# A fused decoder layer on one core: the output products of a pair of heads move between the next head's products, and the first loads and splits are reordered

## The reference

```python
x = x + attn(layernorm(x), W_K, W_Q, W_V, W_O)     # 16 heads of 128, b = 8, pos = 112, d = 512
x = x + xattn(layernorm(x), ctx, Wq, Wk, Wv)
x = x + ffn(layernorm(x), gate, experts, shared)

def attn(x, W_K, W_Q, W_V, W_O):
    k, q, v = (einsum('ihd,bpd->biph', W, x) for W in (W_K, W_Q, W_V))
    s = einsum('biph,biqh->biqp', k, q)
    p = softmax(where(tril, s, -1e10) / sqrt(128))
    z = einsum('biqp,biph->biqh', p, v)
    return einsum('df,bqf->bqd', W_O, z_flat)
```

## Time and profile before

| | us |
|---|---|
| median of 3 runs | 947.93 (947.91 to 949.11) |
| profiled execution, its own time | 951.71 |
| its span | 949.9 |
| PE busy in it | 912.1 (96%) |
| DVE busy | 599.3 (63%) |
| ACT busy | 467.5 (49%) |
| POOL busy | 203.6 (21%) |

### The profile page before, as it was taken

How to read it: one execution, slowest core, us unless ns; L and a number is a source line. 1 busy time by engine, 2 the same in 40 slices (tenths; PEclk the granted TensorE clock), 3 DMA queues, 4 the chain that set the end, 5 groups by cost and what they waited for, 6 DMA issues and landing times.

```text
span 949.9 us, 17943 instructions
## 1 busy us (share of the span) xinstructions
PE 912.1 (96%) x7192; PEld 794.1 (84%) x7192; DVE 599.3 (63%) x1299; ACT 467.5 (49%) x1113; POOL 203.6 (21%) x147
## 2 busy tenths in 40 slices
PE   7989999999999999999999999999999999999995
PEld 6978989898989898877777777777878887999994
DVE  5975656566656553675645546545457866888882
ACT  4443333333333323546666666666576234565651
POOL 0242323232323223501011011011000610221222
PEclk9999999999999999999999999999999999999998
DMA  5210091202020203221201010010032685999973
GB/s 182 79 45 23 1 299 36 89 1 89 2 89 1 89 23 105 73 69 67 67 23 34 2 34 23 13 34 13 2 116 80 222 254 185 347 298 277 318 191 48
DMA packets 30754, 93.60 MB, mean 99 GB/s; under 512 B 6112, under 2 KB 9424, under 8 KB 28752
## 3 DMA queue, kind: packets, MB, share of 16 engines
q1 hardware_dynamic: 26368, 83.27, 25.6%
q0 software_dynamic: 4304, 9.19, 5.1%
HBM read 73.80 MB, written 16.81 MB: 95 GB/s over the span
## 4 chain that ended last, share of the span: by engine, by line
PE 70%; DVE 12%; DMA 12%; issue 3%; ACT 2%; POOL 1%; SPq 0%; POOLq 0%; DVEq 0%
PE bank L554 19%; PE bank L555 18%; PE bank L556 18%; DMA out<-yg,meta 11%; PE bank L801 3%; PE bank L818 3%; PE bank L630 2%; PE bank L655 2%; PE bank L768 1%; POOL out L2306 1%; PE bank L642 1%; DVE nm L1644 1%; DVE sm L1641 1%; PE bank L828 1%; PE bank L671 1%
## 5 line engine op out<-in xcount | busy, mean ns | idle before, releaser
L1293 ACT ACTIVATE ee<-bank 125x448 f32<-125x448 f32 x192 | 91.0, 547 | 22.0 <-PE bank L801 21.0
L554 PE MATMUL bank<-wkv_hi,ctx_hi 128*125 128x512 f32 x192 | 80.3, 418 | 2.7 <-DVE kn L1795 2.1
L1538 DVE TENSOR_TENSOR E_lo<-F,E_hi 128x940 fp32r<-128x940 f32 (+3 forms) x62 | 80.5, 1320 | 3.5 <-ACT E_hi L1065 3.5
L2197 POOL TENSOR_TENSOR wqk_lo<-wqk_f,wqk_hi 128x1024 fp32r<-128x1024 f32 x15 | 36.9, 2463 | 194.0 <-ACT wqk_hi L1065 194.0
L2197 POOL TENSOR_TENSOR ctx_lo<-ctx_f,ctx_hi 128x500 fp32r<-128x500 f32 x24 | 30.4, 1266 | 219.9 <-ACT ctx_hi L1065 219.9
L555 PE MATMUL bank<-wkv_hi,ctx_lo 128*125 128x512 f32 x192 | 76.0, 396 | 0.0
L556 PE MATMUL bank<-wkv_lo,ctx_hi 128*125 128x512 f32 x192 | 75.7, 394 | 0.0
L1804 DVE COPY kT<-bank 128x250 f32<-128x250 f32 x48 | 20.0, 417 | 84.9 <-PE bank L768 84.8
L554 PE MATMUL bank<-wv_hi,xT_hi 128*112 128x256 f32 x256 | 73.1, 285 | 0.0
L556 PE MATMUL bank<-wv_lo,xT_hi 128*112 128x256 f32 x256 | 72.2, 282 | 0.0
L555 PE MATMUL bank<-wv_hi,xT_lo 128*112 128x256 f32 x256 | 72.2, 282 | 0.0
(11 more groups left out here) (390 smaller groups left out, 2615.5 us busy)
## 6 DMA issues: line engine op xcount, KB each, us to landing
F<-wexp SPq DMA_DIRECT2D x14, 1408.0 KB, 8.3
F<-wexp SPq DMA_DIRECT2D x14, 768.0 KB, 8.0
wqk_f<-wqk SPq DMA_DIRECT2D x16, 512.0 KB, 4.3
ctx_f<-ctx SPq DMA_DIRECT2D x24, 250.0 KB, 2.7
slots<-zt SPq DMA_DIRECT2D x1, 5397.0 KB, 22.1
xg<-slots SPq DMA_DIRECT2D x21, 256.0 KB, 7.4
wv_f<-wv SPq DMA_DIRECT2D x8, 512.0 KB, 5.5
wo_f<-wo SPq DMA_DIRECT2D x8, 512.0 KB, 3.6
```

The lines of the kernel that those rows point to most:

```text
L554: e.matmul(out, a[0], b[0], start=first, stop=False)
L1293: e.activation(ee[(4 * n + r) % 8][:, :], SX[r][0:MS, 0:4 * T], ACT.Exp, scale=0.25).then_inc(*x_exped.did((n, r)))
L1538: return e.tensor_tensor(out, src, high.bitcast(F32), ALU.subtract)
L2197: return e.tensor_tensor(out, src, high.bitcast(F32), ALU.subtract)
```

## The change

The output product of a pair is no longer begun behind the pair's second `z_pe`. Its first three tiles stand behind the first two of the seven products of the iteration after, its other four where they were; DVE's sum of those two products becomes a function of its own, `first_sum`, ahead of the three `o_add`. In iteration 13 nothing can be put between: there `z_pe(13)` and `z_low(13)` are moved ahead of the scores and the shift of head 14. In the start, x is loaded as seven transfers of one tile in place of three (1, 3 and 3 tiles), and the value weights follow the fourth; ACT's `wv_hi` stands behind `first_root(1)`; DVE's `first_low(0)` and `first_scale(1)` stand ahead of its `wv_lo`, and `wqk_lo(0)` ahead of `first_low(3)`; `warm(24)` becomes `warm(30)`. The low part of head 1's weights goes from POOL to DVE, and POOL's `wo_low(0)` behind its `wv_low(1)`. DVE's `tx_low(2)` and `tx_low(3)` move from ahead of `normalise(0)` into iteration 0, around `normalise(1)`.

```diff
         def during(h):
+            q = qk_uses(h + 1)
             if h % 2:
-                return [("v", (h + 1) // 2, b) for b in (4, 6)]
-            return [("o", h // 2 - 1, j) for j in range(3, NA)] if 0 < h < 14 else []
+                return q + [("v", (h + 1) // 2, b) for b in (4, 6)]
+            o = [("o", h // 2 - 1, j) for j in range(NA)] if 0 < h < 14 else []
+            return q[:2] + o[:3] + q[2:] + o[3:]
...
-            warm(24)
+            warm(30)
...
             for h in range(NH - 1):
+                pair_o = 0 < h < 14 and h % 2 == 0
                 if h + 1 in SEVEN:
-                    for i in ORDER:
+                    for i in ORDER[:2]:
                         product_pe(h + 1, i)
+                    if pair_o:
+                        o_pe(h // 2 - 1, range(3))
+                    for i in ORDER[2:]:
+                        product_pe(h + 1, i)
+                    if pair_o:
+                        o_pe(h // 2 - 1, range(3, NA))
...
-                elif 0 < h < 14:
-                    o_pe(h // 2 - 1, range(3, NA))
                 turn_p(h)
+                if h == 13:
+                    z_pe(h)
                 scores_pe(h + 1)
-                z_pe(h)
-                if h % 2:
-                    o_pe(h // 2, range(3 if h < 13 else NA))
-                elif h < 14:
+                if h != 13:
+                    z_pe(h)
+                if h == 13:
+                    o_pe(6, range(NA))
+                elif h % 2 == 0 and h < 14:
                     v_pe(h // 2 + 1, (0, 2))
...
             first_hi(0)
             first_root(1)
+            wv_hi_act(0)
             first_rows(1)
...
+            def first_sum(h):
+                w.wait_ge(*scored[h - 2, 1])
+                w.wait_ge(*pj_act["p", h, 1])
+                w.wait_ge(*pj_full["p", h, 2])
+                e.tensor_tensor(qk[h % 2][:, 0, 0:HT], part[0][:, :], PJ["p", h, 2][:, 0:HT], ALU.add).then_inc(*pj_dve.did(("p", h, 2)))
...
+            first_low(0)
+            first_scale(1)
             w.wait_ge(*wv_hi[0])
             low(wv[1][:, :, :], wv_f[:, :, :], wv[0][:, :, :]).then_inc(*wv0_lo.did(0))
-            first_scale(1)
-            first_low(0)
...
-            tx_low(2)
-            tx_low(3)
             normalise(0)
             for h in range(NH - 1):
+                pair_o = 0 < h < 14 and h % 2 == 0
                 if h + 1 in SEVEN:
+                    first_sum(h + 1)
+                    if pair_o:
+                        o_add(h // 2 - 1, range(3))
                     sums(h + 1)
...
+            def x_load(j):
+                e.dma_start(xa[:, j, :], x_d[j]).then_inc(*x_in[j].did(0))
 
             x_load(0)
             e.dma_start(ident[:, :], ident_d).then_inc(*id_in.did(0))
-            x_load(1)
+            for j in range(1, 4):
+                x_load(j)
             wv_load(0)
             wqk_load(0)
-            x_load(2)
+            for j in range(4, NA):
+                x_load(j)
```

More of the change, by code:

```diff
@@ L293, in qk_uses, with during @@
             return [("p", h, i) for i in ORDER] if h in SEVEN else [("qk", h, n, j) for n, j in QK]
-        def within(h):
+        def during(h):
+            q = qk_uses(h + 1)
             if h % 2:
-                return [("v", (h + 1) // 2, b) for b in (4, 6)]
-            return [("o", h // 2 - 1, j) for j in range(3, NA)] if 0 < h < 14 else []
+                return q + [("v", (h + 1) // 2, b) for b in (4, 6)]
+            o = [("o", h // 2 - 1, j) for j in range(NA)] if 0 < h < 14 else []
+            return q[:2] + o[:3] + q[2:] + o[3:]
         def behind(h):
-            if h % 2:
-                return [("o", h // 2, j) for j in range(3 if h < 13 else NA)]
-            return [("v", h // 2 + 1, b) for b in (0, 2)] if h < 14 else []
+            if h == 13:
+                return [("o", 6, j) for j in range(NA)]
+            return [("v", h // 2 + 1, b) for b in (0, 2)] if h % 2 == 0 and h < 14 else []
         def by_act(u):
@@ L311, in decoder_layer @@
         for h in range(NH - 1):
-            pj_uses += qk_uses(h + 1) + within(h) + [("z", h, g) for g in range(2)] + behind(h)
+            pj_uses += during(h) + [("z", h, g) for g in range(2)] + behind(h)
         pj_turn = len(pj_uses)
@@ L427, in decoder_layer @@
         chain = {n: Chain(stack.enter_context(nc.semaphore("own_" + n))) for n in ("act", "dve", "pool")}
-        x_in = [lane(f"x{g}", [0]) for g in range(len(FIRST))]
+        x_in = [lane(f"x{j}", [0]) for j in range(NA)]
         id_in, mask_in = lane("ident", [0]), lane("mask", [0])
@@ L464, in decoder_layer @@
         GH = [(h, g) for h in range(NH) for g in range(2)]
-        wqk_hi, wqk_lo, wqk0_lo = sig("wqk_hi", range(NH)), sig("wqk_lo", range(1, NH)), sig("wqk0_lo", [0])
+        wqk_hi, wqk_lo, wqk0_lo = sig("wqk_hi", range(NH)), sig("wqk_lo", range(2, NH)), sig("wqk0_lo", range(2))
         wv_hi, wv_lo, wv0_lo = sig("wv_hi", range(NH // 2)), sig("wv_lo", range(1, NH // 2)), sig("wv0_lo", [0])
@@ L570, in qk_pe @@
                 u, p = ("qk", h, n, j), wqk[h % 2]
-                w.wait_ge(*(wqk_lo[h] if h else wqk0_lo[0]))
+                w.wait_ge(*(wqk_lo if h > 1 else wqk0_lo)[h])
                 w.wait_ge(*xT_done[1][3 * n + 3])
@@ L1194, in scalar @@
             first_rows(0)
-            wv_hi_act(0)
             first_hi(0)
             first_root(1)
+            wv_hi_act(0)
             first_rows(1)
@@ L1202, in scalar @@
             wqk_hi_act(0)
-            first_root(2)
             first_hi(2)
             first_hi(3)
+            first_root(2)
             first_rows(4)
@@ L1605, in full @@
                     w.wait_ge(*pj_full["p", h, i])
[L1607 to L1611, removed]
                 full(6)
@@ L1677, in first_stats @@
             def first_stats(i):
-                w.wait_ge(*x_in[[a <= i < b for a, b in FIRST].index(True)][0])
+                w.wait_ge(*x_in[i][0])
                 stats(1, i, 128, xa[:, i, :])
@@ L1691, in first_scale, with wqk_low @@
                 e.scalar_tensor_tensor(rt[1][:, a:b], mv[:, a:b, 0], -1.0, y, ALU.mult, ALU.mult).then_inc(*scaled1.did(g))
+            def wqk_low(h):
+                w.wait_ge(*wqk_hi[h])
+                low(wqk[h][1][:, :, :], wqk_f[h][:, :, :], wqk[h][0][:, :, :]).then_inc(*wqk0_lo.did(h))
             def first_low(i):
@@ L1703, in vector @@
                 first_stats(i)
+            first_low(0)
+            first_scale(1)
             w.wait_ge(*wv_hi[0])
             low(wv[1][:, :, :], wv_f[:, :, :], wv[0][:, :, :]).then_inc(*wv0_lo.did(0))
-            first_scale(1)
-            first_low(0)
             first_stats(4)
+            first_low(1)
             first_stats(5)
-            first_low(1)
+            first_low(2)
+            wqk_low(0)
+            first_low(3)
             first_stats(6)
-            first_low(2)
             first_scale(2)
-            first_low(3)
-            w.wait_ge(*wqk_hi[0])
-            low(wqk[0][1][:, :, :], wqk_f[0][:, :, :], wqk[0][0][:, :, :]).then_inc(*wqk0_lo.did(0))
             first_rows(5)
@@ L1722, in vector @@
                 first_low(i)
+            wqk_low(1)
             w.wait_ge(*xT_done[1][NA - 1])
@@ L1752, in vector @@
                     ws_sum(h + 2)
+                if pair_o:
+                    o_add(h // 2 - 1, range(3, NA))
                 if h % 2:
                     v_dve((h + 1) // 2, (4,))
-                elif 0 < h < 14:
-                    o_add(h // 2 - 1, range(3, NA))
                 pt_copy(h)
+                if h == 13:
+                    z_low(h)
                 shift(h + 1)
[L1759 to L1762, removed]
+                if h != 13:
+                    z_low(h)
+                if h == 13:
+                    o_add(6, range(NA))
+                elif h % 2 == 0 and h < 14:
                     v_dve(h // 2 + 1, (0,))
+                if h == 0:
+                    tx_low(2)
                 if h < 14:
                     normalise(h + 1)
+                if h == 0:
+                    tx_low(3)
             to_add = []
@@ L2231, in gpsimd @@
             e.iota(zt[:, 0:1].bitcast(mybir.dt.int32), [[0, 1]], base=NT, channel_multiplier=1).then_inc(*consts_set.did("zn"))
-            wqk_low(1)
-            wo_low(0)
             for h in range(NH - 1):
@@ L2240, in gpsimd @@
                     wo_low(h // 2)
+                if h == 0:
+                    wo_low(0)
                 if h + 2 in SEVEN:
@@ L2319, in wqk_load @@
                 if h > 1:
-                    w.wait_ge(*(wqk0_lo[0] if h == 2 else ws_lo[h - 2] if h - 2 in SEVEN else wqk_lo[h - 2]))
+                    w.wait_ge(*(wqk0_lo if h < 4 else ws_lo if h - 2 in SEVEN else wqk_lo)[h - 2])
                 e.dma_start(wqk_f[h % 2][:, :, :], wqk_d[h]).then_inc(*wqk_in[h % 2].did(h))
@@ L2340, in ctx_load @@
                 e.dma_start(ctx_f[n % 2][:, :, :], ctx_d[n // MC, n % MC]).then_inc(*ctx_in[n % 2].did(n))
```

(13 more changed lines are left out.)

## The result

The changed kernel took 936.51 us (median of 5 runs, 934.96 to 937.96) against 948.2 for the kernel before (5 runs): a ratio of 0.9873, with a 95% interval of 0.9858 to 0.9888. That is 11.7 us less, where 11.6 were forecast; by the interval the gain lies between 10.6 and 13.5 us. Timed once more, in another group of runs, the same two kernels differed by 12.7 us, so part of the close match is chance. The terms behind the sum came out less well than the sum.

What follows compares the result with a forecast made beforehand. PE was busy for 96% of the span, so mainly its idle time or slow clock could be given back; 3.0 + 0.6 - 1.5 + 8.64 + 0.95 = 11.7, say 11.6, off 947.93 gave 936.3 us, range 931.5 to 938.8.

Steps and rivals of the forecast that it cites:

- The sum: Whole kernel: 3.0 + 0.6 - 1.5 + 8.64 + 0.95 = 11.7, say 11.6 us gained, so 936.3 us.
- start, up to head 0's scores: Start: earlier first product and clock staying up bring head 0's products to 19.2; gain 3.0 us, bounds 1.0 and 3.5.
- iteration 0 up to z: Iteration 0: z begins 5.95 us after head 1's products, 6.56 before; gain 0.6 us, bounds 0 and 3.1.
- clock behind the wait: Iteration 0: one unbroken PE wait of 3.6 us brings the lower clock; cost 1.5 us, bounds 0 and 1.65.
- six pairs: Heads 1 to 11: two products of head h + 2 cover PE's 1.44 us wait, six times; gain 8.64 us.
- head 13: Head 13: z ahead of the scores, first transpose to first output matmul 4.6 us instead of 5.57; gain 0.95.
- so that is 1.65 us at most, and I take 1.5: Start: the clock stays up over the 3.3 us low stretch from 14.8 to 18.1; gain 1.5 us.
- The other half: Start: wv_hi starts when the value weights land, so PE's first product comes at 11.9 instead of 13.38; gain 1.5 us.
- the first rival: Iteration 0: POOL does not take its turn inside ws_sum(2); PE's wait 1.1, gain 15.7 us, 932.2; chance 0.17.
- The margin ahead of the third product: Pairs: first_sum frees the bank at about +5.0, third product starts at +6.5; margin 1.5 us, no new wait.
- The base: Profiled execution took 951.71, so 940.1 after; the gain is taken from the median of 947.93, giving 936.3.

Runs made afterwards that it cites:

- the copies first: Changed kernel with head 0's copies of the turned probabilities ahead of head 2's weight sums on DVE and high part on ACT: 932.61 us, ratio 0.9829.
- the pairs alone: Kernel before with only the moved output products (and z ahead of the scores in iteration 13); start, POOL's order, token splits as before: 937.84 us, ratio 0.9876.
- the fastest kernel: Changed kernel with head 0's copies ahead of the weight sums and POOL's first wo_low behind its first ws_low: 932.21 us, ratio 0.9826.

## Why the prediction was right, step by step

**The sum** was right to 0.1 us, but partly by luck: the errors of its terms have both signs, and what is left of them hides in the spread of the medians (11.7 here, 12.7 in the other group). Read against the second profile of the kernel before, whose start is that of two profiles in three, the terms add up to 12.6, and PE is 12.9 us ahead at z of head 15:

| term | forecast | measured |
|---|---|---|
| start, up to head 0's scores | 3.0 | 1.6 (37.39 to 35.82) |
| iteration 0 up to z | 0.6 | 0.8 |
| clock behind the wait | -1.5 | -1.5 gross, -1.0 net |
| six pairs | 8.64 | 10.1 |
| head 13 | 0.95 | 1.1 |

**Start: the step that failed** is "so that is 1.65 us at most, and I take 1.5", the low stretch counted as a standing cost of the kernel before. The earlier trace rows was one execution; in two more profiles with the same start head 0's products begin at 20.5 and 20.8, and filling the gap gained nothing. So the start gave 1.6 us and not 3.0; with the spread of the changed start (18.48 to 19.23) it is 1.3 to 2.3.

The other half has the right times: PE resumed at 11.77 for 11.9, and head 0's products came at 19.21 for 19.2. Its reason is only half right. I wrote that `wv_hi` starts when the value weights land. In the changed kernel it didn't wait for them; ACT came to it late, behind the root for tiles 1 to 3, and that waited for DVE's statistics, which had waited for an x tile:

```profile
7.23 0.69 DVE L1551 BATCH_NORM_STATS2 st<-xa 128x6 f32<-128x512 f32 x1 [0.79 <-DMA xa<-x]
```

```profile
8.97 0.30 ACT L1081 ACTIVATE rstd<-mv,epsc 128x3 f32<-128x3 f32 x1 [0.67 <-DVE mv L1553]
...
9.41 1.04 ACT L1075 ACTIVATE wv_hi<-wv_f 128x1024 fp32r<-128x1024 f32 x1
```

That both would come at 9.4 is luck. In the second profile of the changed kernel the tiles came sooner and `wv_hi` began at 8.79.

**Iteration 0** went as written: z at 52.91 for 53.1, and one addition between POOL's turns. The wait was 3.0 where I wrote 3.6: z came 0.2 earlier, and transposes and scores took 2.63 us (47.14 to 49.77 with the copies first) and not the 2.34 of the earlier trace rows; the rest is the modelled tail of PE's last score. That POOL takes its turn is shown by moving `wo_low`: z came 2.26 us earlier and PE's wait was 2.15 shorter, 2.2 expected. So the first rival, that POOL does not take its turn, is out. That the 0.8 us come from head 1's low part leaving POOL was read off the profiles and not tested by itself.

**The clock behind the wait** fell, and filling the wait took the fall away: shown. What I left out is that the kernel before can have a fall there too (0.51 in its second profile, 0.60 with the pairs alone), partly hidden by its own waits: from z to the next `turn_p` it takes 22.13 us with that fall and 21.72 in the first profile without it, against 23.16 in the changed kernel. So only 1.0 of the 1.5 counts against it. This and the start's 1.4 are one mistake: I placed the fall by one profile.

**The pairs** went all six, with no new wait. The term was mis-sized: 1.69 and not 1.44 each, 1.5 us in all. The row's 1.44 counts from 82.69, the modelled end of z's last matmul, but the next matmul can start before that end: in iteration 1 z started at 80.74 and the next matmul at 84.13, 3.39 later; now the next starts 80.13 - 78.41 = 1.72 later, where z's row ends 1.95 after its start. The margin ahead of the third product held: `first_sum` starts at 84.70 and ends at 85.3, 5.2 after the first product, where I wrote +5.0, and the third product starts without a wait at 86.76, +6.6 for +6.5.

**Head 13**: z begins 1.27 after the first transpose (1.25 forecast), and the output product at 4.65 (4.6).

**The base.** The profiled execution of before (951.71) was 3.5 us above the median. It had the fall in the start, and its end was longer: from z of head 15 at 406.0 to the end 543.9 us, against 542.2 in the changed kernel. So the spans differ by 15.2 us and the medians by 11.7; the medians count.

## What to carry to other kernels

Look at which of two engines that take turns on SBUF operands has work that can wait. In this kernel 2.4 us of POOL work that nobody waited for, put between two of POOL's other low parts, held a DVE addition of 0.41 us for 2.56, so PE for 2.2 us, and brought the clock down as well; moving it behind the next low part gave 3.2 us back.

Three waits of PE merged into one are not always a gain. Here the merged wait of 3.0 us was followed by the lower clock in all five profiles that have it, and useless work put into it gave back 1.65 us. Waits in pieces are no protection, though: three of the four profiles with the old iteration 0 have a fall there too.

To size a gap between matmuls, take the distance of starts with and without it, not the idle time of the row. And take a second profile before an event of the clock, or the landing of a transfer, is counted as a cost.

## What the runs showed of the hardware

The same program falls to the lower clock at different places in different executions: after the start's gap of 2.82 us in the first profile, not after the gap of 2.46 and 2.36 us at the same place in two others, which fell in 53 to 56 us instead. One fall cost 1.4 to 1.5 us of PE's time from z to the next `turn_p` (23.2 against 21.7). Two low stretches on end were seen behind a wait of 3.0 us (`x` in three transfers) and behind waits in pieces (the kernel before with the start's gap filled).

The kernels without long waits mostly spread little (932.3 to 932.7 in four of five runs with the copies first, mean clock 0.996 and 0.997), while those with one had runs at 0.991 to 0.993, 2 us and more above the fastest. The mean clock doesn't explain every run: the fifth with the copies first took 934.76 at 0.996, and one of the fastest kernel 934.4 at 0.997. What made these two slower isn't known.

DVE and POOL took turns on SBUF operands, one instruction each: beside POOL's two successive low parts of 2.4 and 2.5 us DVE's additions took 2.57 and 2.56 us; behind them, 0.41 and 0.43.
